# Selection products and cross scores in row groups of 32 and 64 rows, with reordered lead-ins, in a chain of transformer blocks

## The reference

```python
def mha(x, ctx, ...):                      # 16 heads of 16
    q = (x @ wq + bq).reshape(B, Nq, H, HD)
    k = (ctx @ wk + bk).reshape(B, Nk, H, HD)
    v = (ctx @ wv + bv).reshape(B, Nk, H, HD)
    scores = einsum('bqhd,bkhd->bhqk', q, k) / sqrt(HD)
    if mask is not None:                   # L1's cross-attention only
        scores = where(mask[:, None, None, :], scores, -inf)
    attn = softmax(scores, axis=-1)
    return einsum('bhqk,bkhd->bqhd', attn, v).reshape(B, Nq, D) @ wo + bo
# L1: x += mha(ln(x), ln(x)) + t_sa;  x += mha(ln(x), ctx, mask) + t_ca;  x += mlp(ln(x)) + t_mlp
# L2: x += g_sa * sa(ln(x)*(1+sc)+sh);  x += ca(ln(x), ctx);  x += g_ff * mlp(...)
# L3: x + ca(ada_ln(x), ada_ln(ctx)),  gains from silu(cond) @ W + b
```

## Time and profile before

| | before |
|---|---|
| time, median of 3 runs | 4093.47 us (4093.1 to 4104.8) |
| the profiled execution | 4085.28 us, span 4083.5 us |
| PE, DVE, ACT, POOL busy | 90%, 54%, 58%, 21% of the span |
| mean granted clock of PE | 0.957 |
| costliest groups | exp on ACT 1214.0 us, maxima of self-attention on DVE 1202.1 us, PV on PE 658.9 us |

### The profile page before, as it was taken

The page is one execution under the profiler, slowest core; times in us unless marked ns, Lnnn a source line. Parts: engine busy times, 40 slices in busy tenths (PEclk is TensorE's granted clock), DMA queues, the critical chain, the costliest instruction groups (busy, mean ns, idle before and its releaser), DMA issues.

```text
span 4083.5 us, 66298 instructions
## 1 busy us (share of the span) xinstructions
PE 3686.6 (90%) x20057; PEld 2191.9 (54%) x20057; DVE 2204.8 (54%) x3612; ACT 2366.1 (58%) x4034; POOL 846.3 (21%) x550
## 2 busy tenths in 40 slices
PE   7999998999998989989998989989989899899888
PEld 5776774346434744356436643464347443564366
DVE  4332336843684547643854558436844486438554
ACT  2333335764676457754775457646764577557654
POOL 3222232005102310024004210141023100240051
PEclk8998999999999999999998999999999999999999
DMA  3101002001000010000001010010000100100000
GB/s 128 32 1 32 31 6 67 2 27 32 11 2 12 32 42 2 17 28 26 1 2 32 12 42 2 27 32 12 2 12 32 42 2 17 32 22 2 12 22 22
DMA packets 89415, 92.65 MB, mean 23 GB/s; under 512 B 28499, under 2 KB 77206, under 8 KB 88982
## 3 DMA queue, kind: packets, MB, share of 16 engines
q1 hardware_dynamic: 60158, 63.43, 4.8%
q10 hardware_dynamic: 28952, 25.23, 2.0%
...
## 4 chain that ended last, share of the span: by engine, by line
issue 80%; POOL 17%; PE 1%; POOLq 0%; DVE 0%; DMA 0%; SPq 0%; ACT 0%; ACTq 0%; DVEq 0%
POOL hidl L1775 3%; POOL hidl L1740 3%; POOL x L1766 2%; POOL ql L1793 2%; POOL small L1700 2%; POOL hTl L1707 1%; PE ps L633 1%; POOL kl L1793 1%; POOL W2h L1784 1%; POOL W1h L1784 1%; POOL W2l L1786 0%; POOL W1l L1786 0%; SPq L590 0%; DMA sel_in<-in_sel 0%; DMA qs<-mrow 0%
## 5 line engine op out<-in xcount | busy, mean ns | idle before, releaser
L1347 ACT ACTIVATE probs<-ps 128x512 f32<-128x512 f32 (+1 forms) x2176 | 1214.0, 635 | 377.8 <-PE ps L633 373.2
L1662 DVE TENSOR_REDUCE mxh<-ps 128x2 f32<-128x1024 f32 x1024 | 1202.1, 1219 | 268.6 <-PE ps L633 268.6
L633 PE MATMUL ps<-probs,v 128*32 128x512 f32 (+1 forms) x4864 | 658.9, 614 | 1.4 <-ACT probs L1347 1.4
L633 PE MATMUL ps<-qs,ks 64*128 64x512 f32 x2048 | 529.6, 472 | 0.0
L633 PEld LDWEIGHTS ps<-qs,ks 64*128 64x128 f32 x2048 | 255.0, 185 | 490.8 <-ACT probs L1347 350.2
L633 PE MATMUL ps<-ks,qs 64*128 64x512 f32 x2048 | 413.2, 455 | 112.9 <-DVE mxh L1662 86.9
L1700 POOL TENSOR_TENSOR small<-small 128x4 f32<-128x4 f32 x66 | 68.2, 1034 | 2105.2 <-DVE small L1392 2105.2
L633 PEld LDWEIGHTS ps<-ks,qs 64*128 64x128 f32 x2048 | 194.5, 183 | 316.3 <-DVE mxh L1662 243.0
L1320 ACT ACTIVATE qs<-ps,cols 128x512 fp32r<-128x512 f32 x320 | 214.1, 689 | 80.3 <-PE ps L633 79.2
L633 PE MATMUL ps<-hT,slot 128*128 128x512 f32 x448 | 220.3, 634 | 23.1 <-ACT hT L1139 20.8
L1659 DVE TENSOR_REDUCE mx<-ps 128x4 f32<-128x312 f32 x384 | 164.0, 476 | 141.2 <-PE ps L633 138.9
...
## 6 DMA issues: line engine op xcount, KB each, us to landing
...
```

Source lines behind the costliest of these rows:

```text
L633: return pe.matmul(out, lhsT, rhs, start=start, stop=stop)
L1347: ins = act.activation(dst, src, ACT.Exp, scale=SCALE)
L1662: dve.tensor_reduce(mxh[:, z, t, j // 2, j % 2, :], ps[:, a:a + 2, :], AX.X, ALU.max, negate=True).then_inc(dve_done, M.add(dve_done, name))
```

## The change

**Selection products.** A K step now makes several pairs at once. Pair pp of the four that share 128 features has its heads in rows 32pp to 32pp+31, so its product contracts over these 32 rows alone, and each pair goes to its own bank: first the high parts of all, then the rests. A word of four letters says who evicts each pair (a is ACT, d is DVE, - is not in this step): "aaaa" and "dddd" are four pairs, "aa--" and "--aa" are halves. The mask is replicated to 128 rows, so that each group adds it from its own rows.

**Cross scores.** The keys are stacked in `kc` as they come, without zeros. Each head's product contracts over 64 rows, the two heads of a pair on the two halves of the array. A now has four matmuls of 78 columns into two banks (0 and 1, or 6 and 7) in place of two of 156 into one.

**Maxima.** Each M has two DMAs (one for the even and one for the odd heads), for four heads in a self-attention and for all 16 in a cross-attention, where there were four, and sixteen for the half.

**Order.** The self lead-in has two P ahead of T1; the A part has 20 A's with ten halves and four P or V; V 2 and V 3 come ahead of the first S; R comes after the ninth unit; M comes one A earlier, and units have up to three A's until the old lead of A's is reached. In a cross-attention that follows a self-attention, keys are projected first, o 2, o 3 of the module before stand between, and the queries of the second half, T1 and V are placed between the A's. The MLPs are as they were. The Silu of the condition moves from R of L1sa to the start of the pass.

The core of the diff:

```diff
-    def stack(g, n, k_by):
-        return [k for pair in (2 * g, 2 * g + 1) for k in (("K", "act", "q", pair, n), ("K", k_by, "k", pair, n))]
...
+    def self_lead(tag):
+        put(tag, ("T", 0), ("P", "q", 0, 0), ("P", "k", 0, 0), ("N", 1), ("T", 1), ("P", "q", 1, 0),
+            ("K", "dddd", "q", 0, 0), ("K", "aaaa", "k", 0, 0), ("P", "k", 0, 1), ("P", "q", 0, 1), ("V", 0), ("K", "ddaa", "k", 0, 1))
...
-        put(tag, ("P", "k", 0, 1), ("P", "q", 0, 1), ("V", 1), ("K", "dve", "k", 0, 1), ("K", "dve", "k", 1, 1))
...
+        def halves(which, c, n):
+            return [("K", "aa--", which, c, n), ("K", "--aa", which, c, n)]
+        beside = (halves("q", 0, 1) + [("P", "k", 1, 0), ("P", "q", 1, 1)] + halves("k", 1, 0) + [("P", "k", 1, 1), ("V", 1)]
+                  + halves("q", 1, 0) + halves("k", 1, 1) + halves("q", 1, 1))
...
+        put(tag, ("V", 2))
+        more(first_slot + 2)
+        put(tag, ("V", 3))
+        lead = first_slot + 4
+        more(lead)
...
-            if u < 2:
-                put(tag, ("V", 2 + u))
...
-                more(lead + 2 * (u + 1))
+                more(lead + min(3 * (u + 1), 2 * (u + 1) + 4))
+            if u == NT:
+                put(tag, ("R",), ("add",))
...
+    def cross_lead(tag, before):
+        put(tag, ("T", 0))
+        if before:
+            put(before, ("OT", GROUPS - 1, NH - 1))
+        put(tag, *projections("k", 0))
+        if before:
+            put(before, *[("aT", NH - 1, c) for c in range(KC)])
+        else:
+            put(tag, ("N", 1))
+        put(tag, ("P", "q", 0, 0))
+        if before:
+            put(before, ("o", 2), ("o", 3))
+        put(tag, ("P", "q", 1, 0), *[("T", 1)] * (not before), ("K", "aaaa", "k", 0, 0), ("K", "aaaa", "q", 0, 0),
+            ("K", "aaaa", "k", 1, 0), ("R",))
+    def cross_attention(tag, follow, before):
         maxima = [("A", i // TPH, n, i % TPH, 0) for n in range(NH) for i in range(GROUPS * TPH)]
-        for i, step in enumerate(maxima[:GROUPS * TPH]):
-            put(tag, step, *(beside[i // 2:i // 2 + 1] if i % 2 else []))
-        put(tag, ("M", 0, 0), *maxima[GROUPS * TPH:-6])
-        last = maxima[-6:] + [("M", 0, 1)]
+        put(tag, *maxima[:2])
+        if before:
+            put(tag, ("N", 1), *maxima[2:4], ("T", 1))
+        else:
+            put(tag, *maxima[2:4])
+        put(tag, *maxima[4:6], ("P", "q", 0, 1), *maxima[6:8], ("K", "aaaa", "q", 1, 0), ("P", "q", 1, 1), *maxima[8:12], ("V", 0),
+            ("K", "aaaa", "q", 0, 1), *maxima[12:16], ("add",), ("M", 0, 0), ("K", "aaaa", "q", 1, 1), *maxima[16:24])
+        last = maxima[24:] + [("M", 0, 1)]
...
+def stack_pairs(who, which, c, n):
+    return [(pp, c * (PAIRS // KC) + pp, ("K", which, c * (PAIRS // KC) + pp, n), {"a": "act", "d": "dve"}[w])
+            for pp, w in enumerate(who) if w != "-"]
...
-                        z, _, j0, step = maxima_of(tag, g, n)
+                    for g, n in [(g, n) for g in range(GROUPS) for n in range(NH)] if KIND[tag] == "self" else [(0, 0), (0, 1)]:
+                        z, w, _, step = maxima_of(tag, g, n)
                         sp.wait_ge(act_done, upto(act_done, (tag,) + step))
-                        for j in range(GH):
-                            h = GH * g + j
-                            sp.dma_start(qs[stacked(h % 2, MAXROW, MAXROW + 1), h // 2, n * HALF:(n + 1) * HALF].bitcast(F32),
-                                         mrow[j0 + j:j0 + j + 1, z * HALF:(z + 1) * HALF]
-                                         ).then_inc(maxima_stacked[g][n], M.add(maxima_stacked[g][n], (tag, j), LOADED))
+                        for e in range(2):
+                            sp.dma_start(qs[stacked(e, MAXROW, MAXROW + 1), 2 * g:2 * g + w // 2, n * HALF:(n + 1) * HALF].bitcast(F32),
+                                         mrow[e:w:2, z * HALF:(z + 1) * HALF]
+                                         ).then_inc(maxima_stacked[g][n], M.add(maxima_stacked[g][n], (tag, e), LOADED))
...
+                        if kind == "A":
+                            rings["pairs"] += 1
+                            b = (0, 6)[rings["pairs"] % 2]
+                            return b, (b, b + 1)
                         rings["small"] += 1
-                        many = kind == "A" or KIND[tag] == "mlp" and kind == "o"
-                        b = (0, 1, 6, 7)[rings["small"] % 4] if many else rings["small"] % 2
...
-                        s = SEL[which] + pp
-                        mm(ps[:, b, 0:kn], sel[:, s, :], hi[:, c, part], True, False)
-                        masked = tag == "L1ca" and which == "k"
-                        ins = mm(ps[:, b, 0:kn], sel[:, s + PAIRS // KC, :], lo[:, c, part], False, not masked)
                         if masked:
                             pe.wait_ge(dve_done, upto(dve_done, "mrowb"))
-                            ins = mm(ps[:, b, 0:kn], sel[0:1, NSEL, :], mrowb[:], False, True)
+                        banks = []
+                        for pp, pair, stack, by in stacks:
+                            b, act_was, dve_was = take((tag,) + stack, banks=single(), **{by: (tag,) + stack})
+                            banks.append(b)
+                            pe.wait_ge(act_done, upto(act_done, *act_was))
+                            pe.wait_ge(dve_done, upto(dve_done, *dve_was))
+                            r = slice(2 * HD * pp, 2 * HD * (pp + 1))
+                            mm(ps[:, b, 0:kn], sel[r, SEL[which] + pp, :], hi[r, c, part], True, False)
+                        for (pp, pair, stack, by), b in zip(stacks, banks):
+                            r = slice(2 * HD * pp, 2 * HD * (pp + 1))
+                            if masked:
+                                mm(ps[:, b, 0:kn], sel[r, NSEL, :], mrowb[r], False, False)
+                            mm(ps[:, b, 0:kn], sel[r, SEL[which] + PAIRS // KC + pp, :], lo[r, c, part], False, True
+                               ).then_inc(mm_done, M.add(mm_done, (tag,) + stack))
+                        continue
...
-                                o = pair % 2 * 2 * SP_
-                                ins = mm(ps[:, a, o:o + 2 * SP_], qs[:, pair, tt], kz[:, pair])
+                                o = pair % 2 * SP_
+                                for e in range(2):
+                                    r = stacked(e, 0, STACK)
+                                    ins = mm(ps[:, a + e, o:o + SP_], qs[r, pair, tt], kc[r, pair, :])
...
-                                ins = mm(ps[0:kw, b + e, :], kz[:, h // 2, e, 0:kw], qs[:, h // 2, half])
+                                r = stacked(e, 0, STACK)
+                                ins = mm(ps[0:kw, b + e, :], kc[r, h // 2, 0:kw], qs[r, h // 2, half])
...
-                    elif kind == "R" and tag == "L1sa":
+                    elif kind == "scond":
```

167 lines of the change are left out of this document (64 added, 103 removed).

## The result

The changed kernel takes 4347.68 us (median of 4 runs, 4342.3 to 4366.57) against 4093.96 us (4 runs), a ratio of 1.0622 with a 95% interval of 1.0584 to 1.0659. The forecast was 3931 us with a range of 3865 to 4025, and "slower" had a chance of 4 in 100. It was wrong in sign.

What follows compares the result with a forecast made beforehand. It took PE to bound the lead-ins, DVE close behind, and neither alone the long self-attention S stretch. Terms summed to -40.3 us a pass, -161 over four, from 4093.5 to a forecast of 3931 us, range 3865 to 4025.

Steps and rivals of the forecast that it cites:

- the case on the other side: Self-attention S stretch: waits for banks cost 3.5 us a unit, the pass is 16 us longer, 4157 us; 4 in 100.
- Four row groups side by side: Selection products: four pairs on 32-row groups overlap and take 0.8 us; the no-overlap rival, 4059 us, had 10 in 100.
- the rival that weights of lo wait for hi: Selection products: 0.2 us lost per group, 8.8 us a pass, time 3966 us; 10 in 100.
- Self A stretches: Self-attentions, first A to first S: 28.5 us instead of 35.0 and 33.6, gains of 6.5 and 5.1.
- Self lead-ins: Self-attentions, ahead of the first A: 23.6 us in L1sa and 17.2 in L2sa, gains of 1.4 and 5.8.
- Self S stretches: Self-attentions, from the first S: one more unit and four units with three A's, a loss of 1.6 us.
- Cross-attentions: Whole cross-attentions: gains of 9.3 us each in L1ca and L2ca and 6.1 in L3ca.
- The S units: Cross-attentions: first four units at 2.2 us instead of 2.6 and S at 0.37 instead of 0.58, together -2.9 us.
- The lead-ins: Cross-attentions, ahead of the first A: 14.0 us in L1ca, where it was 28.6, a gain of 14.6; three K groups 2.3.
- Silu at the start: L1sa's lead-in: the Silu, waiting for small loads ahead of the eviction, costs 2.3 us.
- Maxima loads: Cross-attentions: two loads for all heads bring the first S 1.2 us earlier, and the first four units to 2.2 us.
- S stretch gives it back through the banks: Self-attention S stretch: changed bank history adds 0.25 us on 52 units, twice, 26 us a pass, 4035 us; 10 in 100.

Runs made afterwards that it cites:

- b_k32: The kernel before, with selection products over the 32 rows of their pair, one pair at a time (L1ca's masked keys unchanged): 4366.93 us.
- b_s64: The kernel before, with the S products of the cross-attentions over 64 rows in two row groups: 4202.89 us.
- order_alone: The changed kernel with selection products and cross scores back over 128 rows, keeping its order, steps and loads: 4370.62 us, ratio 1.0662.
- lead26: order_alone with 22 A's ahead of the first S in self-attentions and at most two A's a unit: 4384.33 us.
- b_a78: The kernel before, with each cross-attention A as four 128-row products of 78 columns into two banks: 4210.55 us.
- old_a_two: order_alone with cross-attention A's as two products into single banks out of four, and at most two A's a unit in self-attentions: 4392.12 us.
- b_loads: The kernel before, with two maxima loads per M in place of one per head: 4042.96 us.

## Why the prediction was wrong

**The step that failed is the price itself.** Each term took PE's cost per product at a clock of 1.00 and multiplied it. The prediction read the granted clock in the earlier trace rows, corrected for it what it took from there (1.82 at 0.94, and 1.4 us of L1sa's lead-in), and did not ask what the clock would be once the rows at work changed. The runs showed in its place: 32-row selection products alone take L2sa's A stretch from 1.00 to 0.60 and from 33.6 to 50.6 us (b_k32), 64-row S products alone take L1ca's S stretch from 1.00 to 0.64 and from 37.9 to 47.2 (b_s64). Neither the sum nor a rival has it; the case on the other side ("the same waits, but larger") had the right sign for another reason.

**Four row groups side by side** (taken at 0.8 us, bounds 0.57 and 1.8): the overlap was right, and the cautious 0.8 was not needed. Timeline of PE, L2sa's lead-in of the changed kernel, at 2.4 GHz:

```profile
2002.02 0.50 PE L628 MATMUL ps<-qh,sel 32*128 32x512 f32 x4
2002.35 0.40 PE L628 MATMUL ps<-ql,sel 32*128 32x512 f32 x4
2002.58 0.48 PE L628 MATMUL ps<-kh,sel 32*128 32x512 f32 x2
```

Four pairs take 0.56 us, the lower bound. The four low products stand in the groups of the high ones and start 0.33 us behind them, so the rival that weights of lo wait for hi is out: the weights of `ql` begin to load at 2002.12 us, while the `qh` products run from 2002.02 to 2002.52 in the same groups. The Trainium skill (TensorE: Matmul & The Clock Gate, "What overlaps and what doesn't") has weight loads overlap running matmuls only when the row group differs; this trace does not agree. What the forecast missed is the other side of it, which b_k32 shows.

**Self A stretches** (28.5 us each): 36.3 and 37.5. The work was priced rightly, the clock was not. Where the clock is 1.00, an A with a half takes 1.10 us in the changed kernel (starts of A's at 2011.95 and 2013.05), as forecast (1.13), and 1.56 with full-row halves in order_alone (2033.88 and 2035.44). Ten times the difference, taken off the 33.4 us that order_alone needs at 1.00, leaves an estimated 28.8. The 9 us over it in L2sa are the clock.

**Self lead-ins** (23.6 and 17.2 us): 25.1 and 18.7, 1.5 over in each; at the end PE waits 1.3 us for an eviction by DVE.

**Self S stretches** (152 + 1.6): 162 to 163 us from the first S to the last A in the changed kernel and in order_alone. About 3 of these are one unit more, as the prediction has it, and R's 2.1 are in it. Over S and the rest together the two miss by 10 us. The term was sized by DVE's 1.13 us per A. The first units took far more. Timeline of PE, L2sa of the changed kernel:

```profile
2055.90 1.22 PE L628 MATMUL ps<-ks,qs 64*128 64x512 f32 x4 [0.34 <-DVE mxh L1671]
2058.01 0.80 PE L628 MATMUL ps<-ks,qs 64*128 64x512 f32 x2 [0.89 <-DVE mxh L1671]
...
2059.29 1.93 PE L628 MATMUL ps<-probs,v 128*32 128x512 f32 x8
...
2064.42 1.93 PE L628 MATMUL ps<-probs,v 128*32 128x512 f32 x8
```

From the first S to the third PV it takes 19.8 us, against 13.2 before, where V 2 and V 3 are in it as well. Behind that the units stand 3.02 us apart, against 2.97. PE waits for DVE's maxima in the first units, then runs at 1.2 GHz (PV 1.93 us instead of 1.07 in the earlier trace rows). That the waits made the clock fall is argued from their order in the trace; no run took the waits alone away. lead26, with two A's a unit and two more ahead, comes nearest: its first two units take 3.9 and 2.7 us instead of 5.1 and 4.8, and the stretch is at 0.98.

**Cross-attentions** (-9.3, -9.3, -6.1 us): four errors. The S units were to save 2.9 us, some 1.7 of it by S in 64 rows; that form alone cost 7.9 to 10.4 (b_s64). A was priced at 0.45 us by two banks in turn, and its number of products was not priced: cut into four, it costs 5.4 to 6.1 us in the A stretch and 3.1 to 5.9 behind it even in the old order (b_a78, with 128 rows). And 24 A's with little beside them are thin work: with the forms undone (old_a_two) the A stretches are at 0.80 to 0.85 and the order gains nothing. The lead-ins are the fourth, at 22.9, 18.3 and 14.1 us for 14.0, 14.0 and 11.4: three K groups were priced at 2.3 us by PE alone, and take 6.9 in L1ca and 6.1 in L2ca (1839.24 to 1846.10 and 2257.96 to 2264.06), with waits between them, most of them for ACT. The prediction had put the work that moves to ACT at nothing.

**Silu at the start** (2.3 us lost): right, and a little less. The eviction starts 5.1 us after T0, where it was 3.3. ACT, start of the pass in the changed kernel:

```profile
1573.26 0.20 ACT L1298 ACTIVATE scond<-cond 128x2 f32<-128x2 f32 x1 [2.54 <-DMA ctxk<-in_ctx]
1573.37 1.43 ACT L1148 ACTIVATE hT<-ps,cols 128x512 f32<-128x512 f32 x2
```

**Maxima loads**: right in sign, and somewhat undersized. The prediction has 1.2 us ahead of the first S, and the first units at 2.2 us instead of 2.6. At a clock of 1.00, b_loads gains 0.5 to 0.7 ahead of the first S and 2.2 to 2.8 behind it. **S stretch gives it back through the banks**: not seen. The stretches did give back 10 us, most of it in their first units.
